# A two-layer local-attention and recurrent kernel: the norm ahead of the feed-forward stage by transposing, and shifted sequences rounded by VectorE

## What is computed

```python
xn = layernorm(x)
s = recurrence(xn)                    # conv, two gates, scan, W_out, rms
for l in range(2):                    # on xn
    h = shift_token(x)                # features 64..127 come from the token before
    q, k, v = split(h @ wqkv)         # 8 heads of 64
    q, k = rotary(l2norm(q), l2norm(k))
    x = x + attention(q, k, v) @ wo   # windows of 64, looking at the one before
    h = shift_token(x)
    mu, var = h.mean(-1), h.var(-1)
    h = (h - mu) / sqrt(var + 1e-5) * lg + lb
    a, g = split(h @ w1 + b1)         # 341 + 341
    x = x + (a * gelu(g)) @ w2 + b2
out = x0 + s * silu(x)
```

## Time and profile before

| | us |
|---|---|
| median of 3 runs | 1315.2 (1311.35 to 1317.98) |
| the profiled execution | 1315.54 |
| its span | 1313.7 |
| PE busy | 1264.7 (96%) |
| ACT busy | 1162.1 (88%) |
| POOL busy | 1147.3 (87%) |
| DVE busy | 1088.4 (83%) |

### The profile page before, as it was taken

The page is one execution under the profiler, slowest core; times in us unless marked ns, Lnnn a source line. Parts: engine busy times, 40 slices in busy tenths (PEclk is TensorE's granted clock), DMA queues, the critical chain, the costliest instruction groups (busy, mean ns, idle before and its releaser), DMA issues.

```text
span 1313.7 us, 38163 instructions
## 1 busy us (share of the span) xinstructions
PE 1264.7 (96%) x13793; PEld 1011.5 (77%) x13794; DVE 1088.4 (83%) x1883; ACT 1162.1 (88%) x3529; POOL 1147.3 (87%) x840
## 2 busy tenths in 40 slices
PE   7889999999999999899988999999999999999998
PEld 4777888888888887566657788888888888876776
DVE  6788888888888887599877888899988898983777
ACT  4778999999999998787768899999999999998886
POOL 4888999999999998399778999999999999984776
PEclk9999999999999999999998999999999999999999
DMA  5122222222222221011011222221112222110223
GB/s 165 35 74 62 62 62 66 66 62 62 62 70 70 58 50 38 17 32 38 1 29 30 46 46 46 50 50 46 46 46 47 51 52 50 38 39 25 66 79 97
DMA packets 60298, 70.04 MB, mean 53 GB/s; under 512 B 8912, under 2 KB 38288, under 8 KB 60112
## 3 DMA queue, kind: packets, MB, share of 16 engines
q1 hardware_dynamic: 60112, 67.61, 20.5%
HBM read 13.33 MB, written 4.19 MB: 13 GB/s over the span
## 4 chain that ended last, share of the span: by engine, by line
PE 75%; POOL 7%; ACT 6%; DVE 5%; issue 4%; DMA 2%; SPq 1%; ACTq 0%; DVEq 0%; POOLq 0%
PE ps L203 59%; PE ps L268 8%; PE ps L278 3%; PE ps L281 3%; POOL t L1259 3%; ACT P L655 3%; POOL hxr L1259 2%; DVE t L975 1%; POOL P L1259 1%; DMA norm<-X 1%; DVE nm L1006 1%; DVE t L987 1%; ACT sqk L629 1%; DVE sums L994 1%; POOL side L1289 1%
## 5 line engine op out<-in xcount | busy, mean ns | idle before, releaser
L655 ACT ACTIVATE P<-ps,nm 128x128 f32<-128x128 f32 x1024 | 364.2, 384 | 4.2 <-DVE nm L1006 4.1
L203 PE MATMUL ps<-wqkv,hT 128*128 128x512 f32 x1152 | 330.7, 429 | 14.4 <-DVE t L975 10.4
L1259 POOL TENSOR_TENSOR t<-t 128x1024 f32<-128x1024 f32 x128 | 307.5, 2402 | 32.8 <-DVE t L975 30.4
L1259 POOL TENSOR_TENSOR P<-P,rden 128x512 f32<-128x512 f32 x256 | 294.6, 1160 | 31.0 <-DVE rden L1013 28.9
L203 PEld LDWEIGHTS ps<-wqkv,hT 128*128 128x128 f32 x1152 | 217.0, 190 | 92.0 <-issue 28.4
L1259 POOL TENSOR_TENSOR t<-t,rr 128x1024 f32<-128x1024 f32 x128 | 244.0, 1906 | 19.7 <-ACT rr L638 19.3
L655 ACT ACTIVATION_READ_ACCUMULATOR P<-ps,nm 128x1 f32 x1024 | 230.1, 225 | 0.0
L987 DVE TENSOR_TENSOR t<-ps,tabl 128x512 f32<-128x512 f32 x256 | 164.1, 683 | 41.0 <-ACT sqk L629 39.3
L1259 POOL TENSOR_TENSOR hxr<-hxf,hxr 128x512 fp32r<-128x512 f32 (+1 forms) x93 | 130.8, 1434 | 67.9 <-ACT hxr L711 67.8
L1006 DVE TENSOR_REDUCE nm<-ps 128x4 f32<-128x512 f32 x256 | 173.4, 679 | 6.4 <-PE ps L203 6.3
L645 ACT ACTIVATE PT<-ps 128x1024 f32<-128x1024 f32 x128 | 130.5, 1019 | 48.2 <-PE ps L268 47.3
(11 more groups left out here) (140 smaller groups left out, 2548.5 us busy)
## 6 DMA issues: line engine op xcount, KB each, us to landing
Vs<-Vn SPq DMA_DIRECT2D x224, 128.0 KB, 2.3
side<-in_x SPq DMA_DIRECT2D x17, 256.0 KB, 2.9
A<-X SPq DMA_DIRECT2D x16, 256.0 KB, 2.5
norm<-X SPq DMA_DIRECT2D x32, 128.0 KB, 2.2
norm<-X SPq DMA_DIRECT2D x32, 127.8 KB, 2.4
hsh<-X SPq DMA_DIRECT2D x31, 128.0 KB, 2.3
hsh<-X SPq DMA_DIRECT2D x31, 127.8 KB, 2.3
oT<-in_x SPq DMA_DIRECT2D x15, 256.0 KB, 2.9
```

The costliest lines, as they stand in the source:

```text
L203: return e.matmul(o, lhsT, rhs, start=start, stop=stop, skip_group_check=True)
L655: k = act(P[:, g, :], ps[:, 3 + s, (g % 4) * 128:(g % 4 + 1) * 128], ACT.Exp, bias=nm[:, g:g + 1], accum_out=den[:, g:g + 1])
L1259: return e.tensor_tensor(o, a, b_, op)
```

## The change

Per sequence, the two halves of the output projection become one of 512 columns (step 3) with one add. PE transposes the shifted sequence h2 (`turn_h`, step 0), DVE takes mean and variance of every token with batch-norm statistics (`stats_h`, step 1), ACT takes the root of 4 columns (`root_h`, step 1), DVE subtracts and scales out of PSUM (`apply_h`, the last job of step 1), PE transposes back (`turn_back`, step 2) and ACT copies to B (`keep_h`, step 3). The matmuls for mean and variance, `centre`, `scale_hc`, `square_hc`, `log_var`, `root_var` and `side_free` are gone. `shift_hi` goes from POOL to DVE for sequences 3 to 15 of layer 0 and 2 to 15 of layer 1 (step 2, i = 4b-2), and `shift_lo` stays on POOL, in layer 0 two steps later than before (step 3). `ln_stats` is one step earlier, with two buffers for its result.

```diff
-        mv = sb("mv", [128, TPB, 2])
+        mv = sb("mv", [128, 2, TPB, 2])
...
+        def turn_bank(l, b):
+            return 2 if b < NB - 1 else 6 + l
+        def back_bank(b):
+            return 2 if b < NB - 1 else 7
...
-            def proj(l, b, u, bank):
+            def proj(l, b):
+                m = l * NB + b
+                e.wait_ge(s_o, l * NT + 4 * b + 4)
+                if b:
+                    e.wait_ge(s_hn, m)
...
                 for c in range(4):
-                    k = mm(ps[:, bank, 0:256], wo[:, l, c, :], oT[:, c, u * 256:u * 256 + 256], c == 0, c == 3)
+                    k = mm(ps[:, 2, :], wo[:, l, c, :], oT[:, c, :], c == 0, c == 3)
                 k.then_inc(s_wo, 1)
-            def mean(l, b, bank):
-                e.wait_ge(s_h2, 32 * (l * NB + b + 1))
-                mm(ps[:, bank, :], avg, h2[:]).then_inc(s_mu, 1)
-            def var(l, b, bank):
-                e.wait_ge(s_sqh, l * NB + b + 1)
-                mm(ps[:, bank, :], avg, rsd[:]).then_inc(s_va, 1)
+            def turn_h(l, b):
+                m, bank = l * NB + b, turn_bank(l, b)
+                e.wait_ge(s_h2, 32 * (m + 1))
+                if l == 0 and b + 3 < NB:
+                    e.wait_ge(s_x, b + 4)
+                for t in range(TPB):
+                    k = e.transpose(ps[:, bank, t * 128:(t + 1) * 128], h2[:, t * 128:(t + 1) * 128], idf[:])
+                k.then_inc(s_nt, 1)
+            def turn_back(l, b):
+                m, bank = l * NB + b, back_bank(b)
+                e.wait_ge(s_na, m + 1)
+                if l and b + 1 < NB:
+                    e.wait_ge(s_osq, b + 2)
+                for t in range(TPB):
+                    k = e.transpose(ps[:, bank, t * 128:(t + 1) * 128], hn0[:, t * 128:(t + 1) * 128], idf[:])
+                k.then_inc(s_nu, 1)
             def rec_out(b, bank):
                 e.wait_ge(s_hs, b + 1)
+                if b:
+                    e.wait_ge(s_na, NB + b)
+                else:
+                    e.wait_ge(s_b1g, 2)
...
                     if l and (b := hit(i, 6)) is not None:
-                        side_free(l, i - 1)
                         rec_out(b, 2)
...
-                    if (b := hit(i, 5)) is not None:
-                        proj(l, b, 0, 2)
                     if (b := hit(i, 7)) is not None:
-                        proj(l, b, 1, 2)
-                    if (b := hit(i, 8)) is not None:
-                        mean(l, b, 2)
+                        proj(l, b)
+                    if (b := hit(i, 8)) is not None and b < NB - 1:
+                        turn_h(l, b)
                     if (b := hit(i, 10)) is not None:
-                        var(l, b, 2)
+                        turn_back(l, b)
...
+            def root_h(l, b):
+                m = l * NB + b
+                e.wait_ge(s_ns, m + 1)
+                act(nrs, nmv[:, :, 1], ACT.Ln, bias=eps_ln).then_inc(s_nr0, 1)
+                e.wait_ge(s_nr0, m + 1)
+                act(nrs, nrs, ACT.Exp, scale=-0.5).then_inc(s_nr, 1)
+            def keep_h(l, b):
+                e.wait_ge(s_nu, l * NB + b + 1)
+                if l:
+                    e.wait_ge(s_hs, b + 1)
+                act(seq(B, b), ps[:, back_bank(b), :], ACT.Copy).then_inc(s_hn, 1)
...
                     if (b := hit(i, 11)) is not None:
-                        log_var(l, b, 2)
+                        keep_h(l, b)
...
+                    if (b := hit(i, 9)) is not None:
+                        root_h(l, b)
...
                     if b == 1:
-                        square_hc(l, NB - 1)
+                        e.preload_act_table_set(ATTN)
+                        root_h(l, NB - 1)
+                        e.preload_act_table_set(MIXED)
...
+            def shift_hi(l, b):
+                m = l * NB + b
+                e.wait_ge(s_hsh, 32 * m)
+                e.wait_ge(s_vm, 4 * m - 4)
+                e.tensor_copy(hT[:, b % 2, 0, :], hsh[:, b % 2, :]).then_inc(s_hid, 1)
...
+            def stats_h(l, b):
+                m, x = l * NB + b, ps[:, turn_bank(l, b), :]
+                e.wait_ge(s_nt, m + 1)
+                for t in range(TPB):
+                    k = e.bn_stats(nst[:, t, :], x[:, t * 128:(t + 1) * 128])
+                k.then_inc(s_nb, 1)
+                e.wait_ge(s_nb, m + 1)
+                for t in range(TPB):
+                    k = e.bn_aggr(nmv[:, t, :], nst[:, t, :])
+                k.then_inc(s_ns, 1)
+            def apply_h(l, b):
+                m, x = l * NB + b, ps[:, turn_bank(l, b), :]
+                e.wait_ge(s_nr, m + 1)
+                if m:
+                    e.wait_ge(s_nu, m)
+                for t in range(TPB):
+                    k = ts(hn0[:, t * 128:(t + 1) * 128], x[:, t * 128:(t + 1) * 128], nmv[:, t, 0:1], nrs[:, t:t + 1],
+                           ALU.subtract, ALU.mult)
+                k.then_inc(s_na, 1)
...
                     if (b := hit(i, 8)) is not None:
-                        proj_add(l, b, 1, 2)
+                        proj_add(l, b)
+                    if (b := hit(i, 9)) is not None:
+                        stats_h(l, b)
...
+                    if (b := hit(i, -2)) is not None and b >= 3 - l:
+                        shift_hi(l, b)
                     if l == 0:
-                        if (b := hit(i, 12)) is not None:
-                            scale_hc(l, b)
-                        for b in due(i, -7, {0: -1, 1: -1, 2: STATS[2]}):
+                        for b in due(i, -8, {0: -1, 1: -1, 2: STATS[2]}):
                             ln_stats(b)
...
+                    if (b := hit(i, 9)) is not None:
+                        apply_h(l, b)
...
-                        for b in due(i, -3, {0: -1, 1: -1, 2: SHIFT[2]}):
-                            shift_hi(l, b)
+                        for b in due(i, -1, {0: -1, 1: -1, 2: SHIFT[2]}):
                             shift_lo(l, b)
...
             def shift_h2(l, b):
                 m = l * NB + b
-                e.wait_ge(s_xadd, 2 * m + 2)
+                e.wait_ge(s_xadd, m + 1)
...
-                    e.wait_ge(s_hc, m)
+                    e.wait_ge(s_nt, m)
```

More of the change, by code:

```diff
@@ L69, in program @@
         norm = sb("norm", [128, 3 * L])
-        h2, sq, rsd = (norm[:, j * L:(j + 1) * L] for j in range(3))
+        h2, hn0 = (norm[:, j * L:(j + 1) * L] for j in range(2))
         hsh = sb("hsh", [128, 2, L])
@@ L95, in program @@
         cw = [cols[:, 4 + j:5 + j] for j in range(4)]
-        one, eps_ln, eps_rms, ln2x8, mln2, part = (cst[:, i:i + 1] for i in range(6))
-        avg = part.to_broadcast([128, 128])
+        one, eps_ln, eps_rms, ln2x8, mln2 = (cst[:, i:i + 1] for i in range(5))
         ax, ez, u, dd, lnu, ru, half, nx, mx = (ab[:, i:i + 1] for i in range(9))
@@ L108, in program @@
         cv = [side[:, 2, :], oT[:, 3, :]]
+        nst = norm[:, 1280:1304].rearrange("p (t k) -> p t k", t=TPB)
+        nmv = norm[:, 1304:1312].rearrange("p (t k) -> p t k", t=TPB)
+        nrs = norm[:, 1312:1316]
         w1 = norm[:, L:L + 2 * HID]
@@ L142, in program, with rounded @@
         STATS, ROOT, NORM, TURN, SHIFT = {1: 0, 2: 3}, {1: 1, 2: 4}, {1: 1, 2: 5}, {1: 1, 2: 6}, {1: 2, 2: 7}
+        def rounded(l, b):
+            if b < 3 - l:
+                return s_hi, b + 3 * l
+            return s_hid, b - 2 if l == 0 else b - 1 + NB - 3
         def gated(m, j):
@@ L391, in up @@
                     if b == 1 and j == 0:
-                        if l == 0:
-                            e.wait_ge(s_ti, 1)
-                        mean(l, NB - 1, 7)
+                        turn_h(l, NB - 1)
             def down(l, b):
@@ L401, in down @@
                     e.wait_ge(s_w2lo, l + 1)
+                    if l == 0:
+                        e.wait_ge(s_na, NB)
                 if m == 2 * NB - 1:
@@ L566, in ln_root @@
                 e.wait_ge(s_st, b + 1)
-                act(rst[:], mv[:, :, 1], ACT.Ln, bias=eps_ln).then_inc(s_ln0, 1)
+                if b:
+                    e.wait_ge(s_nrm, b)
+                act(rst[:], mv[:, b % 2, :, 1], ACT.Ln, bias=eps_ln).then_inc(s_ln0, 1)
                 e.wait_ge(s_ln0, b + 1)
@@ L715, in conv @@
                 if b == 1:
-                    e.wait_ge(s_wo, 2 * NB)
+                    e.wait_ge(s_wo, NB)
                 elif b:
@@ L937, in first_norm @@
                 for t in range(TPB):
-                    k = ts(xnb[:, t * 128:(t + 1) * 128], tiles(xr[0])[:, t, :], mv[:, t, 0:1], rst[:, t:t + 1],
+                    k = ts(xnb[:, t * 128:(t + 1) * 128], tiles(xr[0])[:, t, :], mv[:, 0, t, 0:1], rst[:, t:t + 1],
                            ALU.subtract, ALU.mult)
@@ L1132, in end_add @@
                 e.tensor_tensor(g, y, x, ALU.add).then_inc(s_eo, 1)
-            for i, v in enumerate((1.0, LN_EPS, RMS_EPS, 8 * LN2, -LN2, 1.0 / D)):
+            for i, v in enumerate((1.0, LN_EPS, RMS_EPS, 8 * LN2, -LN2)):
                 e.memset(cst[:, i:i + 1], v)
@@ L1177, in vector @@
```

(22 more changed lines are left out.)

139 lines of the change are left out of this document (36 added, 103 removed).

## The result

The changed kernel takes 1380.81 us (median of 4 runs, 1380.34 to 1382.46) against 1314.31 us before: 1.0507 times as long, with a 95% interval of 1.0478 to 1.0536. The forecast was 1381.

A forecast was written before the change was run, and what follows sets the result against it. PE, level with a PE and ACT loop, bounds the kernel; 13 layer-0 rounds x 1.6 + 14 layer-1 rounds x 3.3 + 2 x 0.9 = 69, less 3 for absorbed layer-0 stalls: +66 on 1315.2, forecast 1381. Range 1340 to 1402.

The forecast's parts named there:

- The two loops: Regular rounds: a PE and ACT loop of 7.19 us per interval, level with PE; a second over two intervals, 14.77.
- counter-theory C: PE pushes ACT, so relieved intervals shrink with PE's work: 26 us come back, 1289; chance 0.09.
- The projection, +1.7 in interval 3 to 0: From `turn_p` of step 3 to the next step 0, bound by PE: grows to 10.15 (layer 0) and 9.82 (layer 1).
- rival B: Only the projection's move costs: 13 x 0.9 + 14 x 1.2 + 2 = 31, so 1346; chance 0.2.
- `apply_h` and the wait of `rec_out`: Layer 1, interval 1 to 2: PE's `rec_out` stands 1.6 us for DVE's `apply_h` (1.1 us); interval becomes 10.0.
- the sign of being right: PE idle by 3 us per round in layer 1, with a wait of `rec_out` on `apply_h` of 1 to 2 us.
- The loops in layer 0: Late `stats_h` makes interval 0 to 1 7.55; two-step loop adds 14.77: 22.3 to step 3, round 32.5, +1.6.
- Interval 2 to 3 of layer 1: DVE's rounding and `rec_gamma` ahead of `rotate`, after a late `keep_k`: 0.5 late, interval 7.7.
- The ends of the layers: Last sequence's norm in the feed-forward loop: PE gains 0.8, longer last projection costs 1.7, +0.9 per layer.
- The rounding on DVE: 27 copies leave POOL for DVE, 0.6 us assumed each; worth 0 to 13 us, POOL's relief gives nothing back.
- rival D: Copy and POOL block each other, some 0.9 us more for each of 27 copies: 24 more, 1405; chance 0.07.
- `shift_lo` in step 3 at nothing: Layer 0: `shift_lo` stands behind `ln_apply` in step 3, the interval that has 10 us for POOL; no cost.

The follow-up runs named there:

- run 1: Kernel before, with every sequence's mean and variance matmul replaced by one cheap bf16 identity matmul: 1314.19 us against 1316.82, ratio 0.9979.
- Run 2: Kernel before, with only the two halves of the output projection merged into one of 512 columns in step 3, one add: 1355.46 us, ratio 1.0280.
- Run 6: Changed kernel with only two of the four weight blocks of the output projection: 1336.46 us, ratio 1.0140 to the kernel before.
- Run 8: Changed kernel with `apply_h` ahead of `norm_sum` in step 1 instead of behind it: 1369.12 us, ratio 1.0386 to the kernel before.
- run 7: Changed kernel with half of the output projection's weight blocks and the rounding back on POOL at its old places: 1325.72 us, ratio 1.0061 to the kernel before.

## Why the prediction was right

- *The two loops.* This step carried the forecast, and run 1 is its direct test: some 40 us of PE's work for 2.8 us of time. The counter-theory C (26 us faster) falls with it.
- *The projection, +1.7 in interval 3 to 0.* Measured 1.72 (10.17 against 8.45) and 1.79 (9.91 against 8.12). Run 2 gives 1.028 (+37) for the merge alone against 1346 (+31) in rival B's sum. Its rounds grow by 1.2 us in layer 0, where B had 0.9, since the two-step loop makes interval 1 to 2 7.5 and not 7.2, and by 1.6 in layer 1, where B had 1.2, since interval 2 to 3 is 7.51; the ends of the layers give the rest. Run 6 shows it from the other side.
- *`apply_h` and the wait of `rec_out`.* Forecast 1.6 us each, measured 1.64 and 24.8 in 15 waits. PE is idle for 3.1 us per round of layer 1 (36.8 of the 415.6 us of 12 rounds), where "3 us" was the sign of being right. `apply_h` takes 1.36 and not 1.1, because one tile out of PSUM takes 404 ns where the row of the kernel before, out of SBUF, had 340. Run 8 shows that the wait's cause is the place of `apply_h`.
- *The loops in layer 0.* The three intervals 0 to 3 were forecast at 22.3 together and are 22.35, but shared out otherwise: `stats_h` ahead of `keep_k` costs 0.15, not 0.35, and the two-step loop takes 15.1 instead of 14.77.
- *Interval 2 to 3 of layer 1* is 7.24, not 7.7. The copy takes 0.4, not 0.6; the rest of the difference was not taken apart. Interval 1 to 2 is 0.3 longer than forecast, so that the round agrees to 0.1: two errors that cancel.
- *The ends of the layers*: forecast +0.9 each, measured +5.3 after layer 0 and +0.6 after layer 1. Too small by 4. The trace shows something that the sum left out: in the first 10 us after the last `turn_p` of layer 0 the granted clock was 0.83, and 20 us on, behind a stop of 3.37 us, it was 0.66, where the kernel before had 1.00 in this stage. Nine matmuls of 128x512 took 4.18 us there (from 569.81), and 2.64 at full clock 12 us later. My counts for the loops, 18 and 46, were too large by 3 against 16.6 and 44.6, which hides it in the sum. That the forecast of 1381 was met to the microsecond is luck of this kind; that it came near is not.
- *The rounding on DVE.* "0 to 13 us" holds in the changed kernel (7 us), and rival D (over 1.2 us for a copy) is out: none took more than 0.83. So a copy that met a `normalise` lost 0.43 us and not a whole instruction of 1.04. But the reasoning was incomplete. I looked for the price of the copy and saw that `scale_hc` meets POOL at 0.4 us. I did not see that the same meeting can last 4.9 us, and that moving POOL's subtraction by two steps shifts when `scale_hc` starts. In the changed kernel this did not matter, since the norm removes `scale_hc` in the same change; the forecast named neither the danger nor that escape, so its right number for this part is luck.
- *`shift_lo` in step 3 at nothing*: true as said, with the cover named (10 us in that interval). Run 6 shows the bound of 8.9 that appears when the cover goes, and run 7 that it goes with this edit.

The parts do not add up. Alone on the kernel before, the merge costs 37 us and the rounding 61, already more than the 67 of the whole. An edit's price belongs to the kernel in which it is made.

## What to carry to other kernels

An engine that is busy for 100% of a stretch may still be level with a dependency loop. Cut the stretch into its intervals and follow one loop through the other engines; work taken from an interval at its loop's length gives nothing, and work merged into the longest interval costs its full length. Where PE waits for a buffer inside a step, everything behind it waits too, so the reader of that buffer belongs as early in its own engine's step as its inputs allow. Before moving work to or from POOL, look for VectorE instructions with two SBUF operands: what they cost depends on whether POOL leaves a pause. A stop of PE can cost more than its length: here 3.1 us cost up to 2.8 us more, where the granted clock was lower behind it.

## What the runs showed of the hardware that I had not expected

A VectorE `tensor_tensor` of 128x512 with both operands in SBUF (`scale_hc`) took 0.68 us where POOL was idle, 1.08 to 1.23 in most meetings with one POOL instruction, 2.2 to 2.4 when it met two, and 4.86 when it started during an add of POOL that was followed by three more instructions without a pause. VectorE did not get its turn between them. In the kernel before both outcomes occur from the same start, 0.37 us into the first of two `normalise`: at 300.01 it took 1.22, and the two took 2.49; at 144.51 it took 2.22, and the two ran through in 2.04. What decides it was not found. A fp32 to float32r copy of 128x512 from SBUF to SBUF takes VectorE 0.40 us, less than POOL's 0.62 to 0.67, and 0.82 or 0.83 when it meets a `normalise`.
